# Cross-attention block of a perceiver kernel: the mask is prepared by ScalarE instead of VectorE and GpSimd, its first chunk laid by VectorE instead of a transfer, the context loaded in two halves

## The chip, the cores and the metric

The kernel runs on one core of a Trainium2 chip. The metric is the device time of one execution in microseconds; lower is better. The core has TensorE (PE in the rows, with its weight loads as PEld), VectorE (DVE), ScalarE (ACT), GpSimd (POOL) and SyncE (SP), which here only issues transfers.

## The reference, cut to what matters

For a batch of 32, `x` is 64 x 256 per entry and the context is 1601 x 256 per entry, float32. The model is a layer norm, masked cross-attention of `x` on the context with 16 heads of 16 columns, a residual; then causal self-attention with a gate; then a layer with 8 experts. The change touches the cross-attention alone:

```python
qp = (q @ Wq.T + bq).reshape(b, t_q, h, d // h).transpose(0, 2, 1, 3)
kp = (k @ Wk.T + bk).reshape(b, t_kv, h, d // h).transpose(0, 2, 1, 3)
vp = (v @ Wv.T + bv).reshape(b, t_kv, h, d // h).transpose(0, 2, 1, 3)
scores = jnp.einsum('bhqd,bhkd->bhqk', qp, kp) / jnp.sqrt(jnp.float32(d))
mask = (attention_mask == 1)[:, None, :, :]
scores = jnp.where(mask, -jnp.inf, scores)
attn = jax.nn.softmax(scores, axis=-1)
out = jnp.einsum('bhqk,bhkd->bhqd', attn, vp)
```

The mask is int32, 64 x 1601 per batch entry, with values 0 and 1; a position with 1 is excluded.

## The kernel before

**Blocks and periods.** The cross-attention is a software pipeline over the 32 batch entries, called blocks. In the period of block b each engine works on three blocks: scores, exponentials and values of block b; key and value projections and the maxima of block b+1; and the loading and splitting of the context and the mask of block b+2. Two periods form the body of a hardware loop (periods 2 to 29); the rest stands unrolled around it.

**Orders.** The order of work in a period is written by hand in five lists, one for each engine, and every engine works strictly in the order of its list. A letter is a kind of unit and the number says which one. On TensorE, S is half a tile of transposed scores (8 products; 13 tiles of up to 128 context rows make 26 units), K one of 8 key projections, M one of 16 products from which the maxima are taken, V one of 7 value projections (V6 has half the work), W the values of one tile (W11 and W12 also sum the weights, and W12 adds the sums that GpSimd made), T the turning of the maxima into a row, O the turning of the previous block's output. On ScalarE, E is the exponential of one S, KH and VH keep the results of K and V, CH makes the float16 high part of one of the four context chunks. On GpSimd, A1 to A10 add up the exponentials of tiles 0 to 10, CL makes the low part of a context chunk, QB spreads the queries, MQ makes the last chunk of the mask. On VectorE, X is the maximum of one M, KL the low part of K, SH gathers the maxima, SPR writes the row of shifts that every S of the block reads, MP makes the first three mask chunks, MA1 to MA3 copy mask chunk 1 to 3 into the stacked keys for all 16 heads, N normalizes the previous block and R adds the residual. On SyncE, CX loads the context and the mask, QR and QS bring the queries, MD0 lays mask chunk 0 by a transfer, ST0 and ST1 stack the two halves of the keys (17 transfers each).

**The places the change touches.** `mbias` holds the mask as bfloat16, minus 2^120 at a masked position and zero elsewhere, in two buffers. It is made by `prepare_mask` on VectorE (L517, columns 0 to 1151) and by `mask_tail` on GpSimd (L387, the last 449 columns). It is read twice: by every X (L496) and, as raw 16-bit numbers, by `lay_mask`, which copies 64 partitions of it into the stacked keys `kst`. Chunks 1 to 3 are copied by VectorE (L523) and chunk 0 by a transfer (L343).

The first S of a block waits for SPR (`qaug_ready`), for chunk 0 of the mask (`laid[0]`) and for the first half of the stacked keys. The first key projection K0 waits for all four CL of its block, and so for GpSimd's CL3 in the period before. `BANK` gives each unit its PSUM bank, and a unit waits until the unit that used the bank before has been read. M3 uses the banks of K3 and K4, so it waits for KL4, which waits for KH4; KH4 may overwrite the keys only when ST1 of the block before has landed.

## Time and profile before

| | |
|---|---|
| time, median of 3 runs | 2209.67 us (2206.32 to 2211.14) |
| time of the profiled execution | 2218.2 us |
| its span | 2216.4 us |
| start of the first and the last product of the values (L749), by the trace | 116.5 and 1563.3 us |
| busy in the steady stretch from 200 to 1400 us: PE, DVE, ACT, POOL | 1026.3, 867.9, 713.5, 959.1 us of 1200 |
| mean granted TensorE clock in that stretch | 0.93 |

The busy share of TensorE says little by itself, since its products overlap in the pipeline. The useful views here are the list of waits, which says what ended the idle time of an engine, and the timeline of each engine around the point where one period ends and the next begins. A releaser "issue" means that the engine waited for nothing that the profile shows.

### The profile page before, as it was taken

The page shows a single profiled execution, that of the slowest core. Times are in us where ns is not written, and L with a number is a line of the kernel's source. Part 1 is how long each engine was busy: PE and PEld are TensorE (multiplying, and loading weights), DVE is VectorE, ACT ScalarE, POOL GpSimd, SP SyncE. Part 2 cuts the span into 40 slices and gives each one's busy share as a digit, 9 for nine tenths or more (in the row PEclk, how much of TensorE's full clock was granted, in tenths as well). Part 3 has the DMA queues.
Part 4 walks back from the last instruction along what each step waited for, and adds up shares of the span by engine and source line. Part 5 has one row for each costly group of instructions (what it writes and reads, how often), then busy time and mean ns, then how long its engine had stood idle before and what let it go on. Part 6 is the DMA issues. An engine that isn't in the chain of part 4 may idle for free. (4 is left out here: it accounts for less than half of the span.)

```text
span 2216.4 us, 63044 instructions
## 1 busy us (share of the span) xinstructions
PE 1827.9 (82%) x24267; PEld 1300.9 (59%) x24267; DVE 1476.4 (67%) x3029; ACT 1124.7 (51%) x1815; POOL 1446.3 (65%) x714
## 2 busy tenths in 40 slices
PE   2687888888888888888888888888768787599996
PEld 1365656655666566655666555666435555388885
DVE  3676768766777776776777777778567776544442
ACT  2365655665666565555656566655354442133332
POOL 3387778877888787878778788886345541144442
PEclk9999999999999998989999999999885655699998
DMA  3567766677666776667766677664353333377774
GB/s 108 126 129 144 134 124 121 124 146 130 124 120 127 143 137 116 124 121 148 132 120 123 119 144 137 122 122 83 113 181 132 110 101 121 124 231 221 231 220 134
DMA packets 198496, 302.86 MB, mean 137 GB/s; under 512 B 60020, under 2 KB 166324, under 8 KB 197955
## 3 DMA queue, kind: packets, MB, share of 16 engines
q1 hardware_dynamic: 189412, 286.90, 58.7%
q0 software_dynamic: 8832, 12.06, 2.8%
q8 instruction: 223, 3.65, 0.8%
q14 instruction: 29, 0.24, 0.0%
HBM read 163.02 MB, written 31.98 MB: 88 GB/s over the span
## 5 line engine op out<-in xcount | busy, mean ns | idle before, releaser
L399 POOL TENSOR_TENSOR p_sum<-p_sum,pT 128x1024 f32<-128x1024 f32 x288 | 678.4, 2355 | 207.9 <-ACT pT L616 195.5
L616 ACT ACTIVATE pT<-scored,lift 128x512 f32<-128x512 f32 (+1 forms) x832 | 546.9, 684 | 206.3 <-PE scored L726 187.7
L496 DVE CUSTOM_DVE_ANT_0 junk<-key_ring,mbias 128x898 bf16<-128x898 f32 (+1 forms) x512 | 508.7, 1021 | 197.7 <-issue 197.3
L726 PE MATMUL scored<-qst,kst 128*128 128x64 f16 x6656 | 333.0, 199 | 105.0 <-issue 97.1
L726 PEld LDWEIGHTS scored<-qst,kst 128*128 128x128 f16 x6656 | 283.8, 103 | 206.1 <-issue 165.4
L373 POOL TENSOR_TENSOR cp<-cx,cp 128x768 f16<-128x768 f32 (+1 forms) x128 | 318.0, 2492 | 60.4 <-ACT cp L574 60.4
L692 PE MATMUL key_ring<-wvp,cp 128*128 128x256 f16 (+1 forms) x2496 | 317.3, 277 | 1.4 <-DVE kl L469 0.6
L603 ACT ACTIVATE kh<-key_ring,bks 128x384 f16<-128x384 f32 (+1 forms) x256 | 152.4, 595 | 252.6 <-PE key_ring L681 181.7
L692 PEld LDWEIGHTS key_ring<-wvp,cp 128*128 128x128 f16 (+1 forms) x2496 | 232.5, 100 | 59.2 <-issue 20.4
L749 PE MATMUL o_acc<-pT,v 128*32 128x128 f32 x6656 | 261.4, 288 | 2.1 <-DVE x_all L485 0.9
L469 DVE SCALAR_TENSOR_TENSOR kl<-key_ring,bks,kh 128x384 f16<-128x384 f32 (+1 forms) x256 | 162.4, 635 | 132.8 <-ACT kh L603 128.1
L523 DVE COPY kst<-mbias 64x6144 f16<-64x6144 f16 (+1 forms) x96 | 219.5, 2287 | 3.0
L681 PE MATMUL key_ring<-cp,wkr 128*128 128x384 f16 (+1 forms) x768 | 185.7, 382 | 31.8 <-issue 31.4
L749 PEld LDWEIGHTS o_acc<-pT,v 128*32 128x32 f32 x6656 | 174.3, 114 | 56.5 <-issue 31.6
L624 ACT ACTIVATE v<-key_ring 128x512 f32<-128x512 f32 (+1 forms) x224 | 125.7, 561 | 154.1 <-PE key_ring L692 154.1
L681 PE MATMUL key_ring<-cp,wkp 128*128 128x384 f16 x768 | 161.4, 350 | 36.0 <-POOL cp L373 33.9
L1558 POOL DMA_INDIRECT acc_d<-ys,to_row x46 | 74.8, 1625 | 158.8 <-DVE ys L1672 151.8
L1753 PE MATMUL score<-xp,w1p 128*128 128x256 f16 x1518 | 175.9, 275 | 2.3 <-DVE xp L1650 1.6
L984 POOL TENSOR_TENSOR w_parts<-w_whole,w_parts 128x1408 f16<-128x1408 f32 x24 | 70.8, 2957 | 140.9 <-ACT w_whole L1254 140.9
L1753 PEld LDWEIGHTS score<-xp,w1p 128*128 128x128 f16 x1518 | 147.6, 99 | 25.2 <-issue 7.5
L707 PE MATMUL key_ring<-kh,qh 32*128 32x384 f16 x512 | 119.3, 347 | 43.6 <-DVE kl L469 33.8
L681 PEld LDWEIGHTS key_ring<-cp,wkr 128*128 128x128 f16 x768 | 72.1, 106 | 92.0 <-issue 53.3
(224 smaller groups left out, 2438.6 us busy)
## 6 DMA issues: line engine op xcount, KB each, us to landing
cx<-in_ctxT SPq DMA_DIRECT2D x32, 1601.0 KB, 14.3
w1p<-wsp SPq DMA_DIRECT2D x23, 1408.0 KB, 8.5
msk<-in_mask SPq DMA_DIRECT2D x64, 400.2 KB, 14.0
kst<-mbias SPq DMA_DIRECT2D x32, 768.0 KB, 14.5
wsp<-w_parts SPq DMA_DIRECT2D x24, 704.0 KB, 3.7
w2p<-wsp SPq DMA_DIRECT2D x23, 640.0 KB
kst<-kh SPq DMA_DIRECT2D x256, 52.1 KB, 2.3
kst<-kl SPq DMA_DIRECT2D x256, 52.1 KB, 2.3
```

Source lines behind the costliest of these rows:

```text
L373: pool.tensor_tensor(cp[:, j, 1, :, chunk(n)], cx[:, :, chunk(n)], cp[:, j, 0, :, chunk(n)], ALU.subtract).then_inc(cl_ready, 1)
L399: pool.tensor_tensor(p_sum[:], p_sum[:], pT[:, u], ALU.add).then_inc(added, 1)
L469: dve.scalar_tensor_tensor(kl[:, t, chunk(c)], ring[:, BANK["K", k], 0:KWIDTH[c]], bks[:, c % 2, t:t + 1], kh[:, t, chunk(c)], ALU.add, AL ...
L496: dve.tensor_tensor_reduce(junk[:, n % 2, :, 0:MPAIR[half]], ring[:, at:at + 2, 0:MPAIR[half]], mbias[:, j, MS[2 * half]:MS[2 * half] + 2 ...
L523: dve.tensor_copy(kst[MASK_AT:P, :, chunk(c)], mbias[MASK_AT:P, j, MS[c]:MS[c] + KWIDTH[c]].bitcast(F16).unsqueeze(1).to_broadcast([S, H, ...
L603: act.activation(kh[:, t, chunk(c)], ring[:, BANK["K", k], 0:KWIDTH[c]], ACT.Identity, bias=bks[:, c % 2, t:t + 1]).then_inc(kh_kept, 1)
L616: act.activation(pT[0:n, u, HALF * half:HALF * half + HALF], scored[0:n, half, :], ACT.Exp, bias=lift[0:n, 0:1], scale=SSCALE).then_inc(ex ...
L681: mm = pe.matmul(ring[:, BANK["K", k], 0:KWIDTH[c]], (wkp, wkr)[c % 2][:, z, cc, P * t:P * t + P], cp[:, j, y, cc, chunk(c)], start=(cc == ...
L692: mm = pe.matmul(ring[0:n, BANK["V", u], D * half:D * half + D], cp[:, j, z, cc, P * kt:P * kt + n], wvp[:, y, cc, :], start=(cc == 0 and ...
L726: mm = pe.matmul(scored[0:n, half, S * (h % PAIRS):S * (h % PAIRS) + S], kst[:, place, rows], qst[:, j, h, :], start=True, stop=True, skip ...
L749: mm = pe.matmul(o_acc[STRIP * g:STRIP * g + STRIP, P * t:P * t + P], v[0:n, j, kt, STRIP * p:STRIP * p + STRIP], pT[0:n, u, P * p:P * p + ...
L1753: mm = pe.matmul(score[:, 2 * (g % 2) + bank, at], w1p[:, i % 2, c, z, P * block:P * block + P], xp[:, i % 2, y, c, :], start=(c == 0 and ...
```

## The change

The mask is kept with the other sign: plus 2^96 at a masked position, subtracted in X, with the sign of the constant in `delta` turned as well. ScalarE makes it in a unit MB: one instruction Abs(mask - 1) over all 1601 columns in place, then, after that has completed, two instructions Relu(2^96 - 2^96 * that) into `mbias`. MP on VectorE and MQ on GpSimd are gone. Chunk 0 is laid by VectorE as MA0, between SH and SPR, instead of by SyncE's MD0. CX becomes CX0 and CX1, one for each half of the columns, with a semaphore each; CX0 waits only for CL0 and CL1 of the previous use. The mask is loaded by a unit MK of its own after QS. The lists of all engines are rearranged, and some banks are dealt out anew.

```diff
-MASKED = float(2.0 ** 120)
+MASKED = float(2.0 ** 96)
...
-PE_ORDER = steps("S0 K0 S1 K1 O S2 S3 K2 S4 M0 W0 S5 K3 S6 M1 S7 K4 W1 S8 M2 S9 K5 M3 S10 S11 W2 M4 M5 S12 S13 K6 S14 W3 W4 M6 M7 K7 S15  "
-                 "S16 M8 M9 W5 W6 V0 S17 S18 M10 M11 V1 S19 W7 S20 M12 M13 W8 W9 S21 V2 S22 M14 M15 W10 S23 V3 S24 V4 S25 T V5 W11 W12  "
+PE_ORDER = steps("S0 S1 K0 K1 S2 S3 K2 M0 S4 O S5 K3 S6 K4 M1 S7 S8 W0 W1 M2 K5 S9 M3 S10 W2 W3 S11 M4 M5 S12 K6 S13 W4 M6 M7 S14 S15 K7  "
+                 "S16 W5 M8 M9 S17 S18 V0 W6 W7 M10 M11 S19 V1 S20 S21 M12 M13 W8 W9 S22 V2 S23 V3 M14 M15 S24 S25 W10 W11 V4 V5 T W12  "
                  "V6")
-ACT_ORDER = steps("E0 KH0 E1 KH1 E2 E3 E4 E5 KH2 E6 E7 KH3 KH4 E8 E9 KH5 E10 E11 E12 E13 KH6 E14 KH7 CH0 E15 E16 VH0 E17 E18 E19 VH1 E20  "
-                  "CH1 E21 VH2 E22 E23 CH2 VH3 E24 E25 VH4 VH5 CH3 VH6")
-POOL_ORDER = steps("QB A1 A2 A3 A4 A5 A6 A7 A8 CL0 A9 CL1 A10 CL2 CL3 MQ")
-DVE_ORDER = steps("N MA3 R KL0 X0 KL1 X1 KL2 KL3 KL4 X2 X3 KL5 X4 X5 KL6 X6 X7 KL7 X8 X9 X10 X11 X12 X13 MP X14 X15 SH MA2 SPR MA1")
-SP_ORDER = steps("CX QR QS MD0 ST0 ST1")
+ACT_ORDER = steps("E0 E1 KH0 KH1 E2 E3 KH2 E4 E5 E6 KH3 KH4 E7 E8 CH0 KH5 E9 E10 E11 E12 KH6 E13 E14 E15 KH7 E16 E17 E18 VH0 E19 E20 E21  "
+                  "CH1 VH1 E22 VH2 E23 CH2 E24 VH3 E25 CH3 VH4 MB VH5 VH6")
+POOL_ORDER = steps("QB A1 A2 A3 A4 A5 CL0 A6 A7 A8 A9 CL1 A10 CL2 CL3")
+DVE_ORDER = steps("MA3 N KL0 KL1 R X0 KL2 X1 KL3 KL4 X2 X3 KL5 X4 X5 KL6 X6 X7 KL7 X8 X9 X10 X11 X12 X13 MA2 X14 X15 SH MA0 MA1 SPR")
+SP_ORDER = steps("CX0 CX1 QS MK QR ST0 ST1")
...
-        ("T", 0): 2, ("V", 0): 4, ("V", 1): 4, ("V", 2): 4, ("V", 3): 4, ("V", 4): 0, ("V", 5): 4, ("V", 6): 1}
+        ("T", 0): 0, ("V", 0): 4, ("V", 1): 4, ("V", 2): 3, ("V", 3): 4, ("V", 4): 0, ("V", 5): 3, ("V", 6): 2}
...
-                    def load(b):
-
-                        after(sp, cl_ready, KC * b)
-                        sp.dma_start(cx[:], a["ctxT"][bass.ds(b, 1)].rearrange("o (c p) k -> p (o c) k", p=P)).then_inc(ctx_in, 16)
-                        after(sp, mask_ready, b)
-                        after(sp, tail_ready, b)
+                    def load(b, part):
+
+                        after(sp, cl_ready, KC * b + (2 * part + 2 - KC))
+                        sp.dma_start(cx[:, :, HALVES[part]],
+                                     a["ctxT"][bass.ds(b, 1), :, HALVES[part]].rearrange("o (c p) k -> p (o c) k", p=P)).then_inc(ctx_in[part], 16)
+
+                    def load_mask(b):
+
+                        after(sp, mask_ready, 2 * b)
                         for half in range(2):
                             sp.dma_start(msk[64 * half:64 * half + 64, :], a["mask"][bass.ds(b, 1)].rearrange("o q k -> (o q) k")).then_inc(mask_in, 16)
...
-                    def lay_mask(b, j, c):
-
-                        after(sp, st_done, HT * b + (2 * GT * (c + 1) - HT))
-                        if not has_later(b - 1):
-                            sp.wait_ge(mask_ready, b + 1)
-                        sp.dma_start(kst[MASK_AT:P, :, chunk(c)],
-                                     mbias[MASK_AT:P, j, MS[c]:MS[c] + KWIDTH[c]].bitcast(F16).unsqueeze(1).to_broadcast([S, H, KWIDTH[c]])).then_inc(laid[c], 16)
...
-                    def mask_tail(b, j):
-
-                        pool.wait_ge(mask_in, 32 * b + 32)
-                        after(pool, laid[KC - 1], b - 1)
-                        pool.tensor_tensor(hold_p[:], lift[0:1], lift[0:1], ALU.add)
-                        pool.tensor_scalar(mbias[:, j, MS[3]:NM], msk[:, KS[3]:NK], 1, -MASKED, ALU.is_equal, ALU.mult).then_inc(tail_ready, 1)
...
-                        if n % PAIRS == 0:
-                            dve.wait_ge((mask_ready, tail_ready)[n // PAIRS], b + 1)
+                        if n == 0:
+                            dve.wait_ge(mask_ready, 2 * b + 2)
...
-                                                 1.0, -3e38, ALU.add, ALU.max, mx[:, p, half:half + 1]).then_inc(m_read, 1)
+                                                 1.0, -3e38, ALU.subtract, ALU.max, mx[:, p, half:half + 1]).then_inc(m_read, 1)
...
-                    def prepare_mask(b, i, j):
-
-                        dve.wait_ge(mask_in, 32 * b + 32)
-                        after(dve, m_read, MUNITS * (b - 1))
-                        after(dve, laid[0], 16 * (b - 1))
-                        dve.tensor_scalar(mbias[:, j, 0:MS[2] + KWIDTH[2]], msk[:, 0:KS[3]], 1, -MASKED, ALU.is_equal, ALU.mult).then_inc(mask_ready, 1)
-
                     def lay_mask(b, j, c):
 
-                        dve.wait_ge(*((mask_ready, b + 1) if c < KC - 1 else (tail_ready, b + 1)))
+                        dve.wait_ge(mask_ready, 2 * b + 2)
...
+                        if n % 2 == 0:
+                            act.wait_ge(ctx_in[n // 2], b * 16 + 16)
                         if n == 0:
-                            act.wait_ge(ctx_in, b * 16 + 16)
                             after(act, v_done, VU * (b - 1))
...
+                    def prepare_mask(b, j):
+
+                        act.wait_ge(mask_in, 32 * b + 32)
+                        act.activation(msk[:].bitcast(F32), msk[:], ACT.Abs, bias=less_one[:, 0:1]).then_inc(mask_apart, 1)
+                        after(act, m_read, MUNITS * (b - 1))
+                        after(act, laid[KC - 1], b - 1)
+                        act.wait_ge(mask_apart, b + 1)
+                        for to, cols in ((0, slice(0, KS[3])), (MS[3], slice(KS[3], NK))):
+                            act.activation(mbias[:, j, to:to + cols.stop - cols.start], msk[:, cols].bitcast(F32), ACT.Relu, bias=masked[:, 0:1],
+                                           scale=-MASKED).then_inc(mask_ready, 1)
...
-                            pe.wait_ge(laid[c], b + 1 if c > 0 else b * 16 + 16)
+                            pe.wait_ge(laid[c], b + 1)
...
-    delta[-S:] = MASK_Q * np.eye(S)[:, None, None, :]
+    delta[-S:] = -MASK_Q * np.eye(S)[:, None, None, :]
```

## Rows read from the trace of the kernel before

**Rows 1.** The waits, whole span: us in total, times, longest us.
```profile
PE key_ring L681 <- POOL cp L373: 33.9, 18, 2.3
...
PE key_ring L707 <- DVE kl L469: 33.8, 14, 6.0
...
PE key_ring L681 <- issue: 31.4, 13, 3.4
```
**Rows 2.** PE's timeline from T to K0; start, duration, what, idle before.
```profile
982.79 0.61 PE L769 MATMUL key_ring<-minus,m 128*1 128x128 bf16 x8
983.33 1.48 PE L692 MATMUL key_ring<-wvp,cp 128*128 128x256 f16 x12
984.74 0.64 PE L749 MATMUL o_acc<-pT,v 128*32 128x128 f32 x16
...
985.64 0.62 PE L749 MATMUL o_acc<-pT,v 65*32 65x128 f32 x16
...
987.05 0.84 PE L692 MATMUL key_ring<-wvp,cp 128*65 128x256 f16 x6
987.73 0.40 PE L726 MATMUL scored<-qst,kst 128*128 128x64 f16 x8
990.40 1.69 PE L681 MATMUL key_ring<-cp,wkp 128*128 128x384 f16 x6 [2.27 <-POOL cp L373]
```
**Rows 3.** PE's timeline: inside K7, at S20, V6, first S after the loop's branch.
```profile
1011.39 0.91 PE L681 MATMUL key_ring<-cp,wkr 128*128 128x449 f16 x2 [2.46 <-issue]
...
1020.02 0.41 PE L726 MATMUL scored<-qst,kst 128*128 128x64 f16 x8 [0.40 <-ACT pT L616]
...
1032.18 0.84 PE L692 MATMUL key_ring<-wvp,cp 128*65 128x256 f16 x6
1035.43 0.60 PE L726 MATMUL scored<-qst,kst 128*128 128x64 f16 x8 [2.41 <-issue]
```
**Rows 4.** GpSimd's timeline: A10, CL2 with CL3, MQ; a CL0.
```profile
981.50 2.35 POOL L399 TENSOR_TENSOR p_sum<-p_sum,pT 128x1024 f32<-128x1024 f32 x1
983.80 6.54 POOL L373 TENSOR_TENSOR cp<-cx,cp 128x768 f16<-128x768 f32 x2
...
990.46 2.87 POOL L387 TENSOR_SCALAR mbias<-msk 128x449 bf16<-128x449 int32 x1
...
1020.30 1.67 POOL L373 TENSOR_TENSOR cp<-cx,cp 128x768 f16<-128x768 f32 x1
```
**Rows 5.** VectorE's timeline: SH, MA2, SPR, MA1.
```profile
982.11 0.17 DVE L504 TENSOR_REDUCE m<-mx 128x8 bf16<-128x16 f32 x1
982.31 3.15 DVE L523 COPY kst<-mbias 64x6144 f16<-64x6144 f16 x1
985.50 1.21 DVE L509 TENSOR_SCALAR qst<-key_ring 1x1024 f16<-1x1024 f32 x1
986.74 1.86 DVE L523 COPY kst<-mbias 64x6144 f16<-64x6144 f16 x1
```
**Rows 6.** ScalarE's groups by form: busy us, mean ns, idle before.
```profile
L574 ACT ACTIVATE cp<-cx 128x768 f16<-128x768 f32 x96 | 80.2, 837 | 2.8 <-DMA cx<-in_ctxT 2.8
...
L574 ACT ACTIVATE cp<-cx 128x898 f16<-128x898 f32 x32 | 30.3, 946 | 0.0
```
**Rows 7.** VectorE's groups by form: X of the second half, MP.
```profile
L496 DVE CUSTOM_DVE_ANT_0 junk<-key_ring,mbias 128x898 bf16<-128x898 f32 x256 | 269.7, 1087 | 95.4 <-issue 95.2
...
L517 DVE TENSOR_SCALAR mbias<-msk 128x1152 bf16<-128x1152 int32 x32 | 67.1, 2096 | 0.0
```
**Rows 8.** Line 1301, the self-attention's exponential: ns min/median/max.
```profile
L1301 ACT ACT_TABLE_LOAD  x7: 1283/1283/1283, 1652.0 to 1803.0; - x7
```
**Rows 9.** SyncE's timeline: the context's load.
```profile
994.97 0.40 SPq L302 DMA_DIRECT2D cx<-in_ctxT  x1
```
**Rows 10.** The page's transfers: KB each, us from issue to landing.
```profile
cx<-in_ctxT SPq DMA_DIRECT2D x32, 1601.0 KB, 14.3
...
kst<-mbias SPq DMA_DIRECT2D x32, 768.0 KB, 14.5
```

More of the change, by code:

```diff
@@ L217, in program @@
             lift = sb1("lift", [P, 1])
-            hold_p = sb1("hold_p", [1, 1])
+            less_one = sb1("less_one", [P, 1])
+            masked = sb1("masked", [P, 1])
             hold_v = sb1("hold_v", [P, 2])
@@ L227, in program @@
             xw = pT[:, 0:2].rearrange("p s (c k) -> p s c k", c=DC)
-            ctx_in, ch_ready, cl_ready = sem("ctx_in"), sem("context_high_ready"), sem("context_low_ready")
+            ctx_in = [sem(f"ctx_in{j}") for j in range(2)]
+            ch_ready, cl_ready = sem("context_high_ready"), sem("context_low_ready")
             wp_high, wp_ready = sem("weights_high_parts"), sem("weight_parts_ready")
-            mask_in, mask_ready, tail_ready = sem("mask_in"), sem("mask_ready"), sem("mask_tail_ready")
+            mask_in, mask_apart, mask_ready = sem("mask_in"), sem("mask_less_one"), sem("mask_ready")
             laid = [sem(f"mask_laid{c}") for c in range(KC)]
             q_done, qh_kept, q_kept = sem("q_done"), sem("qh_kept"), sem("q_kept")
-            init_done, N_INIT = sem("init_done"), 6
+            init_done, N_INIT = sem("init_done"), 8
             k_done, kh_kept, k_kept = sem("k_done"), sem("kh_kept"), sem("k_kept")
@@ L348, in period @@
                             if kind == "CX" and has_later(b):
-                                load(b + 2)
+                                load(b + 2, n)
+                            elif kind == "MK" and has_later(b):
+                                load_mask(b + 2)
                             elif kind == "QS" and do_b:
@@ L355, in period @@
                                 stack_keys(b + 1, n)
-                            elif kind == "MD" and do_b:
-                                lay_mask(b + 1, 1 - j, n)
                     sp.wait_ge(init_done, N_INIT)
-                    load(0)
+                    for part in range(2):
+                        load(0, part)
+                    load_mask(0)
                     sp.wait_ge(q_kept, DC * NCH)
@@ L406, in period @@
                                 low_context(b + 2, j, n)
-                            elif kind == "MQ" and has_later(b):
-                                mask_tail(b + 2, j)
                             elif kind == "QB" and has_later(b):
@@ L420, in _ @@
                     pool.wait_ge(q_kept, DC * NCH)
-                    mask_tail(0, 0)
                     prepare_queries(0, 0, 0)
@@ L426, in _ @@
                 def _(dve):
-                    dve.memset(mbias[:, :, MS[2] + KWIDTH[2]:MS[3]], -MASKED).then_inc(init_done, 1)
+                    dve.memset(mbias[:, :, MS[2] + KWIDTH[2]:MS[3]], MASKED).then_inc(init_done, 1)
                     dve.memset(hold_v[:], 0.0).then_inc(init_done, 1)
@@ L433, in _ @@
                     dve.memset(lift[:], LIFT).then_inc(init_done, 1)
+                    dve.memset(less_one[:], -1.0).then_inc(init_done, 1)
+                    dve.memset(masked[:], MASKED).then_inc(init_done, 1)
                     dve.wait_ge(x_in, 16)
@@ L544, in period @@
                                 lay_mask(nb, nj, n)
-                            elif kind == "MP" and has_later(b):
-                                prepare_mask(b + 2, i + 1, j)
                     dve.wait_ge(q_kept, DC * NCH)
-                    prepare_mask(0, 0, 0)
                     periods(dve, period)
@@ L636, in period @@
                                 high_context(b + 2, j, n)
+                            elif kind == "MB" and has_later(b):
+                                prepare_mask(b + 2, j)
+                    act.wait_ge(init_done, N_INIT)
+                    prepare_mask(0, 0)
                     periods(act, period)
```

## The prediction

> **What bounds the kernel now.** The list of waits comes first. TensorE is busy 1026 of the 1200 us of the steady stretch, so what matters is what ends its idle time. Three entries there concern this change [rows 1]: K0 waits for GpSimd's last low part, 33.9 us in 18 times; M3 waits for VectorE's KL, 33.8 us in 14 times; and there are waits that nothing in the profile explains. The timelines of two neighbouring boundaries between periods show where they stand. Going from an even block to an odd one, S0 follows V6 at once, then K0 stands still for 2.27 us until CL3 ends [rows 2, 4]. Going from an odd block to an even one, at the loop's branch, S0 itself starts 2.41 us late for no reason shown, and K0 does not wait afterwards [rows 3]. A third kind is a gap in the middle of one unit, 2.46 us within K7 [rows 3], where no semaphore is waited for: I read it, and the one at the branch, as instructions that are not there yet. The change does not shorten the program, so I leave them as they are.
>
> So in this stretch TensorE's own order sets the pace, and the tail of GpSimd's list sets it at every second boundary. GpSimd does A10, CL2 and CL3 back to back from 981.50 to 990.34 us [rows 4], and K0 starts at 990.40.
>
> **Part 1, what is removed.** MQ costs GpSimd 2.87 us [rows 4], but it stands behind CL3, and GpSimd then waits for exponentials anyway; worth 0. MP costs VectorE 2.10 us on average [rows 7], between X13 and X14; its place is taken by MA2, worth about 0. The transfer MD0 moves 768 KB and lands after 14.5 us [rows 10]; nobody waits for it, since its block starts a whole period later. Less traffic may shorten the waits for the stacked keys (part 4).
>
> **Part 2, GpSimd's tail.** One of the low parts moves out of it: a CL0 of 1.67 us [rows 4] now comes after A5. Also, S21 now stands next to S20, ahead of M12, M13, W8 and W9. From S20 to the end of V6 there were 13.0 us [rows 3], and by the count of products the new S21 ends some 12 us before S0's place at 987.73 [rows 2], at 975.7. An exponential and CH1 of 0.84 us [rows 6] end near 977.3. Then come CL1 1.67, A10 2.35, CL2 1.67 and CL3 near 1.9 (the last from 1.67 by its columns): 984.9 with nothing in between. K0 now stands behind S1, so it is due at 988.1. The margin is 3.2 us where 2.27 us were missing.
>
> What eats this margin is VectorE's copies. The row shows it: MA2 is asked for at 982.31, while A10 runs to 983.85, and takes 3.15 us; MA1, of the same shape, takes 1.86 us [rows 5]. MA2 ends 1.61 us after A10. CL2 and CL3 together take 6.54 us where a CL alone takes 1.67 [rows 4]. So each copy that meets GpSimd stops it for about 1.6 us, or is stopped by it. Three copies (MA2, MA0, MA1) would bring CL3 to 989.7, so between 0 and 1.6 us of K0's wait may stay. Since S0 is late in the same case (part 3), I take all 33.9 us as gone.
>
> The Trainium skill (SBUF — State Buffer, Who interferes with whom) says that a VectorE copy in a two-port mode and a GpSimd instruction take one shared pair of ports as an exclusive lock for the whole instruction, in order of issue. The trace agrees with it in MA2's 3.15 us. It speaks against a fourth copy at this place.
>
> **Part 3, VectorE before SPR.** Before, SH at 982.11 was followed by MA2 and SPR, and SPR ended at 986.71, about 1.0 us ahead of S0 [rows 2, 5]. Now MA0 and MA1 both stand between SH and SPR. M15 comes earlier in TensorE's new order: behind it are two S and W10 (1.1 us, an estimate from W11 without its sums), W11 0.90, V4 and V5 2.82, T 0.54, W12 1.41 and V6 0.68 [rows 2], 7.45 us in all. It ends at 980.3, X14 and X15 of 1.05 us each (269.7 over 256) [rows 7] end near 982.3 and SH near 982.5. T ends at 985.6, so the copies are what SPR waits for. With nothing in the way: 982.5 + 2 x 1.86 + 1.21 = 987.4 [rows 5], just in time for S0 at 987.73. If one copy waits out one CL of 1.67 us, SPR ends at 989.1 and S0 starts 1.3 us late. If both do, it is 990.7 and 3.0 us late. CL2 and CL3 run just there, and I take one, 1.3 us. At the branch, S0 is late by 2.41 us anyway [rows 3], which hides 1.3 us. There are 16 boundaries without a branch: +20.8 us, bounds 0 and 48.
>
> **Part 4, the waits in front of M3.** M3 waits for KL4, and KH4 for the landing of ST1. S25, which lets ST1 start, now has W10 and V4 behind it too, so it comes some 1.9 us earlier against S0 [rows 2], K4 is earlier in the list, and the traffic is lighter. That would remove the 33.8 us [rows 1]. But where M3 does not wait, gaps of the third kind turn up nearby, so I take a third, -11.3 us, bounds 0 and -33.8.
>
> **Part 5, ScalarE.** The trace has no Abs and no Relu. The nearest rows are the copies of 768 and 898 columns, 0.837 and 0.946 us [rows 6], 0.84 ns a column. That gives 1.54 us for 1601 columns, 1.16 for 1152 and 0.57 for 449, in sum 3.3 us. They stand between VH4 and VH5. Behind them wait VH5, VH6 and E0. V4 ends 4.0 us before S0's place (V5, T, W12 and V6 follow [rows 2]), VH4 0.6 us later (from the same 0.84 ns a column), MB 3.3 us after that, VH5 another 0.6 us: 0.5 us behind S0's place. K0, which needs V5's bank, is due 0.7 us behind S0. So the cover is thin: 0.2 us if S0 is on time, 1.5 us with S0 1.3 us late as in part 3. I take 0. If ScalarE were late by more, K0 would wait for the rest. A change of function tables would cost 1.28 us each [rows 8], up to 2.6 us in a period: above the cover by 1.1 us at 16 boundaries, 18 us. No such load stands between Copy, Identity and Exp in the cross-attention, so 18 us is only the bound.
>
> The Trainium skill (ScalarE: Activation LUTs, Table sets: the hidden batching unit) says that relu and abs are in every set. By it, the price is 0; no trace so far shows it for these two.
>
> **Part 6, the context in halves.** CX was issued at 994.97, 4.6 us after CL3 had ended at 990.34 [rows 4, 9], because SyncE had first to issue ST1. So the earlier release of a half buys nothing. What it does buy is that CH0 needs only half of the transfer. CH0 moves from after KH7 to after E8, some 13 us behind S0; the load is issued about 5.5 us behind S0 and half of 14.3 us [rows 10] makes 12.7. That just fits: 0, bound +1 us in each of 30 periods. The extra issue of 0.40 us [rows 9] is hidden.
>
> **Part 7, the start.** ScalarE makes the first mask with nothing to hide it, 3.3 us, and MA0 of 1.86 us [rows 5] stands before the first SPR; about one K covers 1.1 us of it: +4.0 us.
>
> **The sum.** -33.9 + 20.8 - 11.3 + 4.0 = -20.4 us. Against the profiled execution's own 2218.2 us that is 2197.8. The median of the runs is 8.5 us lower, 2209.7, so the forecast there is 2189.3, and I write 2189, 0.9% faster.
>
> **Rivals.** *VectorE's chain becomes the bound (slower).* At each boundary both copies lose to CL2 and CL3. S0 is 3.0 us late without the branch and 0.6 us later than now with it: 16 x 3.0 + 15 x 0.6 = 57; minus 33.9 and nothing for M3, plus 4: +27, 2237. It decides from the point where SPR ends 2.3 us behind V6. For it: the copies stand in exactly the stretch where GpSimd has no pause [rows 4]. Against it: GpSimd's tail is shorter, so A10 and CL2 may be over before MA0. Half-way, with S0 2.15 us late without the branch and 0.3 us with it, it is 34.4 + 4.5 - 33.9 + 4.0 = +9.0, 2219. The rule of the shared ports that the Trainium skill gives (SBUF — State Buffer, Who interferes with whom) is this rival's mechanism.
>
> *All of it comes free.* Copies find GpSimd idle, M3's wait goes whole: -33.9 - 33.8 + 4 = -64, and 2146; with half of part 3's price, 2156. For it: 3.2 us of margin. Against: three copies in a row.
>
> *Nothing moves.* What K0 and M3 stop waiting for turns up as gaps of the third kind, whose places depend on the order: -20 + 20 = 0, 2210. For it: they are the largest entry in TensorE's idle time, and 31.4 us of them stand in K units alone [rows 1].
>
> **Chances.** Forecast 0.44 (its own range 2172 to 2204), all free 0.18, VectorE the bound 0.23, nothing moves 0.15. The range leaves out the ends of the second and third: 2156 to 2222. A measurement of this kernel can tell about 0.2% from no change. Faster: 0.44 + 0.18 and a little of the last, 0.63; within: 0.14; slower: 0.23.
>
> **What the profile would show.** Part 2 is right if K0's wait for GpSimd is gone from the waits. Part 3 is right if S0 behind V6 waits about 1.3 us for VectorE at every second boundary. Part 4: M3's wait for KL is near 22 us. Part 5: ScalarE's new instructions take 3.3 us, with no table load between them. Part 6: CH0 has no wait for the context. The prediction is wrong if S0 waits 3 us, if K0 waits for VH5, or if the unexplained gaps change by more than 20 us.

## The result, and the profile after

The changed kernel takes 2142.93 us in the median of 4 runs (2126.50 to 2155.97), the kernel before 2210.4 us in 4: a ratio of 0.967 over their fast runs, 95% interval 0.958 to 0.977, so 3.3% faster (the medians themselves stand at 0.969). Forecast were 2189 us and a range from 2156 to 2222. The sign was right and the size was not: more than three times the gain came, and the median lies outside the range. The profiled execution took 2138.41 us, its span is 2136.6 us, 79.8 us shorter than that of before.

The page's head after the change:

```profile
span 2136.6 us, 63160 instructions
...
PE 1792.0 (84%) x24267; PEld 1280.2 (60%) x24267; DVE 1543.1 (72%) x3031; ACT 1225.2 (57%) x1911; POOL 1420.9 (67%) x650
```

The list of waits after it, in the columns of [rows 1]:

```profile
PE scored L723 <- DVE qst L500: 83.0, 28, 3.8
...
PE scored L723 <- issue: 47.7, 26, 3.7
...
ACT cp L556 <- DMA cx<-in_ctxT: 17.8, 18, 2.0
...
ACT kh L585 <- DMA kst<-kst: 12.2, 10, 2.1
...
PE key_ring L678 <- issue: 7.0, 9, 1.4
PE key_ring L678 <- POOL cp L372: 6.1, 2, 3.2
```

K0's wait for GpSimd fell from 33.9 to 6.1 us, and M3's wait for KL, 33.8 us before, is not in the list any more. In their place stands one new wait, which is now TensorE's largest: S0 for SPR (L500), 83.0 us. And the gaps without a shown reason, which the forecast held fixed, fell most: 97.1 us in S units and the 31.4 us in K units of [rows 1] made 128.5, and now there are 47.7 + 7.0 = 54.7.

Two kinds have to be kept apart in this sum. The stops of S0 behind the loop's branch were 33.1 us in 13 times; now 8.5 us in 3 times are left under this name, since S0 waits for SPR at the same place. At all other places there were 95.4 us, and there are 46.2: they fell by 49 us.

What these gaps are can be read from the trace. The page's third part has a queue of the kind "instruction":

```profile
q8 instruction: 223, 3.65, 0.7%
```

The trace has the time of each of its packets, 16,384 bytes apiece, 5.8 in a period, so one in 7 to 8 us. In the cross-attention TensorE has 47 stops of over 0.3 us without a reason before, those of S0 left out, and 33 after. Every one of them ends 1.2 to 1.9 us after the end of such a packet, and every stop at the branch 1.9 to 2.2 us after one. In all 18 traces of this document it is 493 stops, 1.2 to 2.4 us after a packet, and 150 stops of S0, 1.8 to 2.7 us after one. So TensorE waits there for its next instructions.

The busy time of TensorE is 1792.0 us for the same 24267 products, where it was 1827.9 (the page of before). The steady stretch from 200 to 1400 us shows where part of this comes from, first before, then after (us, then busy time and instructions of PE, PEld, DVE, ACT, POOL, the granted clock, the transfers' share, GB/s):

```profile
200.00:1400.00 1200.00, 1026.27 (x15734) 722.20 (x15733) 867.85 (x1713) 713.54 (x1167) 959.12 (x440) 0.93 0.70 129
```

```profile
200.00:1400.00 1200.00, 1058.80 (x16774) 748.73 (x16773) 980.85 (x1827) 844.37 (x1325) 1008.17 (x415) 0.95 0.61 120
```

By busy time over products, one takes 1026.27/15734 = 65.2 ns before and 1058.80/16774 = 63.1 ns after, at a mean granted clock of 0.93 and 0.95 of 2.4 GHz. The timeline of TensorE at one boundary without a branch shows where the clock is lost:

```profile
846.40 0.84 PE L689 MATMUL key_ring<-wvp,cp 128*65 128x256 f16 x6
850.46 1.03 PE L723 MATMUL scored<-qst,kst 128*128 128x64 f16 x16 [3.21 <-DVE qst L500]
851.30 2.11 PE L678 MATMUL key_ring<-cp,wkp 128*128 128x384 f16 x6
...
858.11 1.14 PE L678 MATMUL key_ring<-cp,wkr 128*128 128x384 f16 x6
```

K0, two S units behind the 3.21 us of idle, takes 2.11 us, and six products of the same shape take 1.14 us further on. The granted clock was 0.50 from 851.3 to 853.5 us and 1.00 from 858.1 to 859.3 us. So such a gap costs its length and again 1 us or more in the products behind it. Not every one does: at 980.96 us, behind 2.76 us of idle, the clock stayed at 1.00 and K0 took 1.14 us. From the first block's S0 to the last one's, TensorE worked 177 us at the half clock before and 125 us after. Half of the difference, 26 us, is the clock's part of the 36 us of busy time, by estimate; the rest stays open.

The same boundary on VectorE, then on GpSimd:

```profile
842.44 0.17 DVE L495 TENSOR_REDUCE m<-mx 128x8 bf16<-128x16 f32 x1
842.64 6.34 DVE L507 COPY kst<-mbias 64x6144 f16<-64x6144 f16 x2
849.01 1.21 DVE L500 TENSOR_SCALAR qst<-key_ring 1x1024 f16<-1x1024 f32 x1
```

```profile
838.49 3.89 POOL L391 TENSOR_TENSOR p_sum<-p_sum,pT 128x1024 f32<-128x1024 f32 x1
842.33 5.03 POOL L372 TENSOR_TENSOR cp<-cx,cp 128x768 f16<-128x768 f32 x2
```

SH is over at 842.61, as near to S0's place (847.24, the end of V6) as the forecast had it: 4.6 us ahead against 5.2. But MA0 and MA1 together take 6.34 us, where a free one takes 1.86 [rows 5]. CL2 starts 0.3 us before MA0 and takes its usual 1.66 us. Then MA0, CL3 and MA1 take turns, and each waits out the one in front: they are recorded with 2.96, 3.43 and 3.46 us. SPR ends at 850.22, 3.0 us behind V6. A10, in front, took 3.89 us instead of 2.35, since MA2 had gone ahead of it.

The exclusive lock on the shared pair of ports, of which the Trainium skill speaks (SBUF — State Buffer, Who interferes with whom), fits all of these durations.

The mask on ScalarE, its timeline from VH4's end to E0, and its groups by form:

```profile
843.86 1.62 ACT L590 ACTIVATE msk<-msk,less_one 128x1601 f32<-128x1601 int32 x1
845.51 1.82 ACT L595 ACTIVATE mbias<-msk,masked 128x1152 bf16<-128x1152 f32 x2
847.23 0.84 ACT L617 ACTIVATE v<-key_ring 128x512 f32<-128x512 f32 x2
851.25 1.27 ACT L609 ACTIVATE pT<-scored,lift 128x512 f32<-128x512 f32 x2 [3.19 <-PE scored L723]
```

```profile
L590 ACT ACTIVATE msk<-msk,less_one 128x1601 f32<-128x1601 int32 x32 | 51.9, 1622 | 0.0
L595 ACT ACTIVATE mbias<-msk,masked 128x1152 bf16<-128x1152 f32 x32 | 40.2, 1256 | 1.2
L595 ACT ACTIVATE mbias<-msk,masked 128x449 bf16<-128x449 f32 x32 | 20.9, 654 | 0.0
```

It takes 1.62 + 1.26 + 0.65 = 3.5 us by the means, 3.3 were forecast, and it is over before S0 can start. There is no table load in the cross-attention: the trace has one at 1 us and the next at 1556 us.

### The profile page after: what moved, and what is told of

Read it like the earlier page. It is cut to its first block and busy times, and to the rows that moved or that the text cites. A ratio compares the mean times of both kernels' runs of the same rounds, so it can differ in the third digit from the quotient of the medians.

```text
span 2136.6 us, 63160 instructions
## 1 busy us (share of the span) xinstructions
PE 1792.0 (84%) x24267; PEld 1280.2 (60%) x24267; DVE 1543.1 (72%) x3031; ACT 1225.2 (57%) x1911; POOL 1420.9 (67%) x650
## 5 line engine op out<-in xcount | busy, mean ns | idle before, releaser
L391 POOL TENSOR_TENSOR p_sum<-p_sum,pT 128x1024 f32<-128x1024 f32 x288 | 702.0, 2438 | 61.1 <-ACT pT L609 44.8
L723 PE MATMUL scored<-qst,kst 128*128 128x64 f16 x6656 | 318.4, 198 | 141.0 <-DVE qst L500 83.0
L723 PEld LDWEIGHTS scored<-qst,kst 128*128 128x128 f16 x6656 | 266.8, 102 | 242.9 <-issue 185.9
L507 DVE COPY kst<-mbias 64x6144 f16<-64x6144 f16 (+1 forms) x128 | 347.3, 2733 | 3.0
L689 PE MATMUL key_ring<-wvp,cp 128*128 128x256 f16 (+1 forms) x2496 | 305.0, 273 | 4.8 <-DVE mx L487 3.8
L746 PE MATMUL o_acc<-pT,v 128*32 128x128 f32 x6656 | 240.1, 278 | 2.1 <-issue 1.1
L746 PEld LDWEIGHTS o_acc<-pT,v 128*32 128x32 f32 x6656 | 169.9, 110 | 24.4 <-issue 8.7
L388 POOL TENSOR_TENSOR p_sum<-pT 128x1024 f32<-128x1024 f32 x32 | 75.4, 2355 | 164.1 <-ACT pT L609 164.1
L678 PE MATMUL key_ring<-cp,wkp 128*128 128x384 f16 x768 | 171.8, 367 | 8.1 <-POOL cp L372 6.1
L981 POOL TENSOR_TENSOR w_parts<-w_whole,w_parts 128x1408 f16<-128x1408 f32 x24 | 69.8, 2917 | 140.6 <-ACT w_whole L1251 140.6
```

The costliest lines, as they stand in the source:

```text
L391: pool.tensor_tensor(p_sum[:], p_sum[:], pT[:, u], ALU.add).then_inc(added, 1)
L507: dve.tensor_copy(kst[MASK_AT:P, :, chunk(c)], mbias[MASK_AT:P, j, MS[c]:MS[c] + KWIDTH[c]].bitcast(F16).unsqueeze(1).to_broadcast([S, H, ...
L678: mm = pe.matmul(ring[:, BANK["K", k], 0:KWIDTH[c]], (wkp, wkr)[c % 2][:, z, cc, P * t:P * t + P], cp[:, j, y, cc, chunk(c)], start=(cc == ...
L689: mm = pe.matmul(ring[0:n, BANK["V", u], D * half:D * half + D], cp[:, j, z, cc, P * kt:P * kt + n], wvp[:, y, cc, :], start=(cc == 0 and ...
L723: mm = pe.matmul(scored[0:n, half, S * (h % PAIRS):S * (h % PAIRS) + S], kst[:, place, rows], qst[:, j, h, :], start=True, stop=True, skip ...
L746: mm = pe.matmul(o_acc[STRIP * g:STRIP * g + STRIP, P * t:P * t + P], v[0:n, j, kt, STRIP * p:STRIP * p + STRIP], pT[0:n, u, P * p:P * p + ...
```

## The experiments

Ratios are to the kernel before, run on the same chip. "Gaps without a reason" are TensorE's idle times with the releaser "issue". The medians of the kernel before were 2210.6 to 2215.4 us in these series; where two kernels ran on different chips, their ratios are the better comparison.

**spr_early**

```diff
-... X14 X15 SH MA0 MA1 SPR
+... X14 X15 SH MA0 SPR MA1
```

> The changed kernel with VectorE's MA1 moved behind SPR (order SH MA0 SPR MA1). After the change S0 waits for SPR 83.0 us in 28 waits, about 3.2 us at nearly every boundary, behind two copies that took 6.34 us together where one alone takes 1.86. Theory A (those copies are what S0 waits for, and TensorE has no other bound close behind): SPR comes about 3.2 us earlier, the wait falls below 15 us, the kernel gains 50 to 75 us against the changed one, near 2080 us. Theory B (the wait only covers something else that is due at the same time: VH5 behind the mask on ScalarE, CL3 on GpSimd, the stop at the loop's branch of 2.4 us): the wait moves to K0 or to S0 without a reason shown, and the gain is under 25 us, 2120 us or more.

Measured 2126.78 us, ratio 0.965 (0.959 to 0.971). S0's wait for SPR is gone (1.1 us are left), but this stands in the waits instead:

```profile
PE scored L723 <- issue: 81.5, 40, 3.1
...
PE key_ring L678 <- POOL cp L372: 37.5, 14, 5.0
```

K0 waits for GpSimd again, more than before the change, and the stops at the branch, which the wait for SPR had covered, show again: 33.0 us in 13 times. The other gaps without a reason grow from 46 to 60 us. Theory B holds: the wait had covered things that are due almost at the same time. The intervals of the two ratios overlap, so no gain is shown.

**chunk0_by_transfer**: the changed kernel, chunk 0 laid by SyncE as before.

```diff
-SP_ORDER = steps("CX0 CX1 QS MK QR ST0 ST1")
+SP_ORDER = steps("CX0 CX1 QS MK QR MD0 ST0 ST1")
-... SH MA0 MA1 SPR
+... SH MA1 SPR
```

> The changed kernel with mask chunk 0 laid by SyncE's transfer of 768 KB as before, and no MA0 on VectorE; everything else as after the change. Theory A (what the change gained in gaps without a reason came from the lighter traffic): the gaps inside S15, S9 and K7 and the wait of M3 come back, 40 to 60 us; SPR comes 3 us earlier, which gives 50 to 75 back; about even, 2115 to 2150 us. Theory B (the gaps went with the new order of units, the traffic has no part in it): only the gain of SPR stays, 2070 to 2095 us.

Measured 2146.09 us, ratio 0.972 (0.968 to 0.977). It is even with the changed kernel, as theory A had it. S0's wait for SPR is gone; K0 waits 28.5 us for GpSimd, and ScalarE waits for the stacked keys, 62.7 us where it was 12.2:

```profile
ACT kh L595 <- DMA kst<-kst: 62.7, 27, 7.8
```

The nearest kernel is spr_early, which also has one copy between SH and SPR and ran on the same chip: 2126.78 us, 29.5 us of this wait, and 17.2 us of S units waiting for ScalarE, where here there are 42.3. So the transfer costs some 19 us in this list, though the two intervals overlap a little, and it costs them behind the stacked keys: M3's wait does not come back, and the gaps without a reason away from the branch are 66 us against 60.

**mask_by_two**: the changed kernel, mask by VectorE and GpSimd.

```diff
-... X12 X13 MA2 X14      (VectorE)     ... CL2 CL3       (GpSimd)   ... VH4 MB VH5   (ScalarE)
+... X12 X13 MP MA2 X14   (VectorE)     ... CL2 CL3 MQ    (GpSimd)   ... VH4 VH5      (ScalarE)
```

> The changed kernel with the mask made by VectorE (1152 columns, behind X13) and GpSimd (449 columns, behind CL3) again instead of by ScalarE. Theory A (moving the mask mattered little, since ScalarE's 3.3 us and GpSimd's 2.9 us both lay beside other work): VectorE's chain to SPR grows by 2.1 us in front of X14, of which a part shows as a longer wait of S0, 5 to 65 us slower than the changed kernel, 2150 to 2205 us. Theory B (ScalarE's mask stands in the way of VH5 and E0, hidden behind S0's wait): ScalarE's time is given back and the kernel is within 10 us of the changed one, 2133 to 2153 us.

Measured 2176.96 us, ratio 0.984 (0.978 to 0.990). That is theory A: 34 us slower than the changed kernel's 2142.93, 40 us slower than its 2137.42 on this chip. V4 needs the bank of M14, and X14 now stands behind MP and MA2:

```profile
PE scored L731 <- DVE qst L513: 76.1, 24, 3.8
PE key_ring L697 <- DVE mx L500: 57.3, 27, 2.4
```

(The two rows are of the steady stretch.) In the changed list the mask's 2.1 us on VectorE have no cover, and ScalarE's 3.5 us were over before anything needed them. What MQ alone costs was not separated.

**after_traffic**

```diff
+sp.dma_start(spare_d[:], qh_all[MASK_AT:P, 0, 0:KWIDTH[0]].unsqueeze(1).to_broadcast([S, H, KWIDTH[0]])).then_inc(spare_in, 16)
```

> The changed kernel with a transfer of 768 KB in each period that nobody waits for, in the place of the removed one, from the queries to a spare place in memory in the same pieces of 768 bytes. Theory A (traffic delays TensorE's instructions and the stacked keys): the gaps without a reason grow from 50 us in the steady stretch towards the 96 us of before, and the time with its clock by 40 to 70 us, 2180 to 2215 us. Theory B (traffic has no part): within 10 us of the changed kernel, 2133 to 2153 us.

Measured 2141.37 us, ratio 0.970 (0.964 to 0.975); gaps without a reason 46.6 + 10.2 = 56.8 us. In the changed kernel 768 KB more per period at this place cost nothing: theory B. It is a milder load than MD0, though. It is issued 13.1 us behind S0 and lands after 9.4 us, while MD0 in chunk0_by_transfer is issued at 14.5 us and takes 13.8 us, and ScalarE waits only 15.0 us for the stacked keys here.

**orders_only**: the kernel before with the new lists and banks alone (MP in front of MA2, MQ behind CL3, MD0 and one CX as before, no MB, no MA0).

> The kernel before with the lists of TensorE, ScalarE, VectorE and GpSimd and the banks of the changed one, and nothing else of the change: the mask by VectorE (in front of MA2) and GpSimd (behind CL3), chunk 0 by the transfer, the context in one piece. Theory A (the order of the units is what took away M3's wait and the gaps without a reason): most of the gain is there, minus what VectorE's mask costs in front of X14 (34 us, as mask_by_two against the changed kernel), 2150 to 2185 us. Theory B (the order matters little and needs the lighter engines and queues): 2190 us or more.

Measured 2283.78 us, ratio 1.029 (1.025 to 1.033). It is slower than the kernel before. The number lies in theory B's range, which was open above, but neither theory expected a loss. The largest reason is in ScalarE's waits, where before there were 2.8 us for the context, and in what follows on TensorE:

```profile
ACT cp L574 <- DMA cx<-in_ctxT: 209.2, 31, 9.6
...
PE scored L726 <- ACT pT L616: 200.2, 53, 8.3
```

CH0 stands after E8 in the new list, and there the whole context has not landed. E9 and S11 stand behind it; 163 of the 200 us are in front of S11.

**one_load**: the changed kernel, CH0 waits for both halves.

```diff
-if n % 2 == 0:
-    act.wait_ge(ctx_in[n // 2], b * 16 + 16)
 if n == 0:
+    for part in range(2):
+        act.wait_ge(ctx_in[part], b * 16 + 16)
```

> The changed kernel with the context still loaded in two transfers, but CH0 waits for both of them, as it had to with one. Theory A (the load in halves is what lets CH0 stand after E8, and orders_only was slow for the lack of it: there ScalarE stood 165 us for the context): ScalarE waits for the context in front of nearly every E9, S11 stands still behind it, 100 to 160 us slower than the changed kernel, 2240 to 2300 us. Theory B (orders_only was slow for its mask in front of X14 and the transfer of chunk 0): ScalarE waits little, within 20 us of the changed kernel.

Measured 2224.77 us, ratio 1.006 (1.003 to 1.010), beside 2137.42 us and 0.968 (0.963 to 0.972) of the changed kernel on the same chip (after_again): 87 us, in kind theory A, a little less than its range. Of the 3.3% nothing is left. TensorE stands still in front of S11 instead, 106 us, and with that the gaps without a reason nearly vanish, 6.3 + 3.1 us.

```profile
ACT cp L556 <- DMA cx<-in_ctxT: 141.1, 31, 7.8
```

**before_light**

```diff
-sp.dma_start(cx[:], a["ctxT"][bass.ds(b, 1)]...
+n = NK if isinstance(b, int) and b == 0 else 48
+sp.dma_start(cx[:, :, 0:n], a["ctxT"][bass.ds(b, 1), :, 0:n]...
```

> The kernel before, but after the first block each load of the context brings 48 of the 1601 columns (about 50 KB instead of 1.6 MB), so later blocks compute with the first one's context elsewhere; the time of all engines' work is unchanged. Theory A (the gaps inside S9, K7, S15 and S20, which the profile gives no reason for, come because TensorE's next instructions arrive behind the bulk transfers, and M3's wait because the stacked keys do): of 97.1 and 31.4 us without a reason some 35 us stay, those at the loop's branch; M3's 33.8 us fall below 10; 60 to 120 us faster with the clock, 2090 to 2150 us. Theory B (these gaps belong to the program's length and order and not to traffic): the gaps stay within 20 us and the time within 25 us of before.

All loads behind the first bring 3% of the context, and the later blocks compute with the first one's elsewhere.

Measured 2083.15 us, ratio 0.939 (0.934 to 0.944): 132 us faster, past the range of theory A. The gaps in K units are not in the list any more. In S units this is left, 34.2 of the 55.7 us at the branch, and M3's wait is 7.3 us:

```profile
PE scored L727 <- issue: 55.7, 31, 2.9
PE key_ring L682 <- POOL cp L374: 41.9, 18, 3.1
```

**after_light**: the same in the changed kernel, 48 columns of each half.

> The changed kernel with each load of a context half cut to 48 columns after the first block (the results of later blocks are made from the first one's context elsewhere). Theory A: the gaps without a reason behind S15, K5 and S11 (50 us in 28 periods) go, the wait of S0 for SPR stays; 30 to 60 us faster than the changed kernel, 2080 to 2115 us. Theory B: gaps stay; within 15 us of the changed kernel.

Measured 2082.85 us, ratio 0.941 (0.938 to 0.945), 60 us faster than the changed kernel.

```profile
PE scored L724 <- DVE qst L501: 105.1, 31, 3.6
...
PE scored L724 <- issue: 2.4, 6, 0.7
```

The two light kernels take the same time within 0.3 us. Without the bulk of the context's transfers the change is worth nothing: what it takes from K0 and the branch it gives back at S0. Its 3.3% show only where the work lies beside those transfers.

The instruction packets say how. The one that is due at S15 in even blocks, the first to begin later than 13 us behind that block's S0, begins 20.8 us behind it in the kernel before and 14.8 us in before_light (medians of 14 blocks). In the changed kernel it is 17.4 us and in after_light 15.2 us. In the kernel before, the context's load lands at 21.3 us; in the changed one, its second half lands at 17.7 us.

**before_small_md0**

```diff
-sp.dma_start(kst[MASK_AT:P, :, chunk(c)], mbias[...].bitcast(F16).unsqueeze(1).to_broadcast([S, H, KWIDTH[c]]))
+sp.dma_start(kst[MASK_AT:P, 0:1, chunk(c)], mbias[...].bitcast(F16).unsqueeze(1))
```

> The kernel before with its transfer of mask chunk 0 cut to one head of 16, 48 KB instead of 768 KB (the other heads of chunk 0 keep zeros, so masked positions there are not excluded). Theory A (that transfer prolongs the stretch in which TensorE's instructions come late, and the change gained by its removal): the gaps inside K7 (31.4 us in 28 periods), S15 and S20 (28 us) go, those inside S9 stay, 25 to 70 us faster than before. Theory B (it costs nothing, as the extra transfer in after_traffic did): within 10 us of before.

Measured 2185.03 us, ratio 0.989 (0.986 to 0.993), 26 us faster: at the lower edge of theory A in size. K7's gap did not go: in the steady stretch K units still have 29.5 us without a reason, where they had 30.4, while M3's wait fell from 23.6 to 9.4 us. So the step that the theory named was the wrong one, and the packet in front of S15 is hardly earlier, 20.4 us. The stacked keys profit: ScalarE's wait for them fell from 69.8 to 40.8 us. Only one head of 16 gets chunk 0 of the mask here, so masked positions there count in the others.

**before_mask_later** and **after_mask_first**: the place of the mask's load, in both kernels.

```diff
-SP_ORDER = steps("CX QR QS MD0 ST0 ST1")            # before; CX loads the mask too
+SP_ORDER = steps("CX QR QS MK MD0 ST0 ST1")
-SP_ORDER = steps("CX0 CX1 QS MK QR ST0 ST1")        # changed
+SP_ORDER = steps("CX0 CX1 MK QS QR ST0 ST1")
```

> The kernel before with the mask's load moved behind the queries (CX QR QS MK MD0). Theory A: the gaps inside S9 and K7, 67.6 us in 28 periods, fall by 20 us or more, 20 to 50 us faster than before. Theory B: within 8 us of before, 0.3% to either side.

> The changed kernel with the mask's load directly behind the context's two, ahead of the queries (CX0 CX1 MK QS QR). Theory A (2.4 MB issued at once hold back TensorE's instructions for longer than 1.6 MB and then 0.8 MB, and the change gained by putting the queries between them): the gaps inside K5 and S15 grow by 20 us or more in 28 periods, 20 to 40 us slower than 2140. Theory B (the place of the mask's load has no part): within 8 us.

In the kernel before, the later load gives 2190.57 us, ratio 0.988 (0.983 to 0.993), 22 us faster. The packet in front of S15 begins at 17.5 instead of 20.8 us. The gaps in K units fall from 31.4 to 8.0 us, and those at S15 from 16.9 to 0.4; part of it comes back at S20, 34.7 us where there were 10.1:

```profile
PE scored L732 <- issue: 96.2, 38, 3.3
...
PE key_ring L687 <- issue: 8.0, 5, 2.5
```

In the changed kernel the earlier load gives 2149.28 us, ratio 0.967 (0.962 to 0.973). The ratio is that of the changed kernel itself, so no loss is shown, though its profiled execution has 57.4 instead of 47.7 us in S units. The packet in front of S15 begins at 17.7 us, where it was 17.4.

**shifted_pages**

```diff
+if j == 0:
+    for _ in range(SPARE_WAITS):        # 60
+        pe.wait_ge(init_done, N_INIT)
```

> The changed kernel with 60 waits on TensorE at the start of every even block that are long satisfied; they do no work. Theory A (the gaps stand at fixed places of the instruction stream, some 240 instructions of product and weight load apart, and mean that the next stretch of instructions isn't there): the gaps that stood behind the fifth product of S15 and the third of K5 in even blocks, and the second of S15 in odd ones, move some 30 products forward, into S13 or W4 and into W0; their sum stays within 20 us. Theory B (they belong to what S15 and K5 wait for): they stay where they are.

Measured 2138.57 us, ratio 0.966 (0.960 to 0.972). The gaps moved. In even blocks of the changed kernel one stands inside S14/S15, with 13 of 16 products in front of it (first row, a short one; 11 of them make 20.8 us). Now none is left there, and one stands inside W4, 5 of 16 products in front (second row, of this kernel, of the same block):

```profile
999.65 0.25 PE L723 MATMUL scored<-qst,kst 128*128 128x64 f16 x3 [0.17 <-issue]
```

```profile
1000.38 0.63 PE L747 MATMUL o_acc<-pT,v 128*32 128x128 f32 x11 [1.19 <-issue]
```

By the new list that is 28 products earlier, and nothing that W4's sixth product could wait for is new. In odd blocks it is the same: from the third product of S15 to the third of W4. In the loop of both kernels, before and after, the places within one block lie 118 to 122 products apart, or twice that, and each product has a weight load. So the gaps belong to places in the instruction stream: theory A. With the packets and before_light it says what they are: TensorE has used up its instructions, and the next ones arrive late while bulk transfers are under way.

Theory A's second part did not come: away from the branch the gaps should have kept their sum within 20 us, and only 15 of 47 us are left. The 60 waits lengthen S0's stop in even blocks from 3 to over 6 us, about 45 us in sum, and the time is the same. Like one_load, this kernel has few gaps because TensorE stands still elsewhere in the period. A shorter list of gaps is therefore no gain by itself.

The rule that the Trainium skill gives fits this (Runtime: NRT & Kernel Launch, Instruction fetch mechanics): instructions are fetched in blocks of 256 by the engine's own transfers. The distance of some 120 products with their weight loads, and the waits between them, agrees. It calls the cost mostly hidden; here it was not, by the 95.4 and 46.2 us.

**spr_early_k_by_half**

```diff
-if k == 0:
-    pe.wait_ge(cl_ready, b * KC + KC)
+if k % (KPROJ // 2) == 0:
+    pe.wait_ge(cl_ready, b * KC + (KC if k else 2))
```

> spr_early, and K0 waits for the low parts of chunks 0 and 1 only, which are all that K0 to K3 read, and K4 for all four. In spr_early K0 waits 32.0 us for GpSimd's last CL, in 12 waits. Theory A (that wait is the bound that took S0's place): it goes, 2085 to 2105 us. Theory B (something else, VH5 behind the mask or VectorE's KL chain, is due at the same time): K0 or K3 waits for that instead, 2115 us or more.

Measured 2122.60 us, ratio 0.958 (0.954 to 0.962), the lowest ratio found. Its interval lies just below that of after_again (0.963 to 0.972), and overlaps that of the first series (0.958 to 0.977). K0's wait went; in the steady stretch O waits for N instead:

```profile
PE o_acc L759 <- DVE att L468: 32.7, 15, 3.0
```

**norm_first**: N ahead of MA3 again.

> spr_early_k_by_half with N ahead of MA3 on VectorE, as in the kernel before. There O waits 32.7 us for the normalization, which stands behind MA3's copy of 2 us. Theory A (that is now the bound in front of O): the wait goes, 20 to 35 us faster than 2122.6. Theory B (TensorE waits for its instructions right after instead, since the page behind K1 is due 8 us later whatever is in front): S9 or K5 take the gap, within 10 us.

Measured 2120.50 us, ratio 0.961 (0.957 to 0.965). O's wait is gone, K3 waits 27.3 us for KL0 instead (steady stretch), and the time is the same: neither theory's gap, but theory B's time.

**late_ma3**: MA3 behind X0.

> norm_first with MA3 behind X0 instead of behind N. In norm_first K3 waits 27.3 us for KL0, behind MA3's 2 us. Theory A (MA3 is what it waits for): that wait goes, 10 to 25 us faster, 2095 to 2110 us. Theory B (K3 is early and another wait follows, for its instructions or for the exponentials): 2113 us or more.

Measured 2133.79 us, ratio 0.963 (0.958 to 0.968), no gain. That is theory B. K3's wait fell to 3.2 us, and the M units behind X0 wait for VectorE:

```profile
PE key_ring L704 <- DVE mx L487: 51.2, 35, 3.2
```

**after_again** is the changed kernel in a second series.

> The changed kernel as it is, on the chip of the three others of this call, for comparison with them: 2130 to 2155 us, 0.96 to 0.975 of the kernel before.

It took 2137.42 us, ratio 0.968 (0.963 to 0.972).

## Why the prediction was right or wrong

The terms against the profiled executions (us):

| term | forecast | measured |
|---|---|---|
| K0 waits for GpSimd | -33.9 | 33.9 to 6.1: -27.8 |
| S0 waits for SPR | +20.8 | 83.0 |
| M3 waits for KL | -11.3 | -33.8 |
| gaps without a reason | 0 | 128.5 to 54.7: -73.8 |
| TensorE's busy time | 0 | 1827.9 to 1792.0: -35.9 |
| start of the first values | +4.0 | 116.5 to 124.5: +8.0 |
| sum | -20.4 | -80.3 (span: -79.8) |

That the measured column closes is no proof of causes: busy and idle time of TensorE make up the span whatever ended the waits. The rows of S0 and of the gaps also share the stops at the branch. Taken by place, S0 waited 35.6 us for all reasons before and 91.5 us after, +55.9, and the other gaps are -49.2.

**The step that failed** is the last sentence of the first part: that the third kind of gap belongs to the program's length and is to be left as it is. It stands in the sum as 0. I had read it rightly as instructions that are not there yet, and the packets and shifted_pages bear that out. But when they arrive depends on the transfers, which before_light shows, and whether TensorE is there first depends on the lists. The gaps' own -73.8 us hold 24.6 us at the branch, which now lie under S0's wait; so 49 us are real. With fewer idle times goes part of the 36 us of busy time, for which the sum had no term at all, though the profile of before showed the price: it lists K units of 1.69 and 2.10 us behind a gap and 1.14 us elsewhere.

**The right sign was luck.** The terms that the sum did have, measured, are -27.8 for K0, +55.9 for S0, -33.8 for M3 and +8.0 for the start: +2.3 us, no gain. All of the gain is in the two terms that were put at nothing. It is luck too that the rival "all of it comes free" had 2146 us: it needs copies that find GpSimd idle, and they did not.

**Part 1**, MD0 worth nothing: wrong in the kernel before, 26 us by before_small_md0, and likely in the changed one, some 19 us by chunk0_by_transfer against spr_early. MP for MA2 worth nothing: that exchange was not tested by itself; with MP in front of MA2 and MQ back, the new list loses 34 us.

**Part 2**, K0's wait: right in size, but not by the margin of 3.2 us. In spr_early, where S0 is not late, K0 waits 37.5 us for GpSimd, longer than the 33.9 us of before. The wait was covered by S0's, not removed. GpSimd's A10 and its CL wait for VectorE's copies as priced.

**Part 3**, SPR: its mechanism was right, its size mis-sized. I took one collision of two, 1.3 us, and both happen, 3.0 us. Without the branch S0 waits 41.2 us in 15 times, inside the bound of 48. With the branch it waits 50 us where it was 36, so the branch hides most of it but not all. In the list both stand under SPR: 83.0 us in 28 waits. The rival "VectorE's chain becomes the bound" had this wait nearly and was still wrong in its sum, for want of the two missing terms.

**Part 4**, M3: all of it went, not a third. It stays away in chunk0_by_transfer and in orders_only too, so the new lists removed it, not the missing transfer. ScalarE's wait for the stacked keys fell from 69.8 us (waits of before) to 12.2. Of this, chunk 0 is worth some 33 us (62.7 against 29.5 in spr_early). Another 17 us is the difference between spr_early and the changed kernel, where S0 starts later.

**Part 5**, ScalarE: right, 3.5 us for 3.3, hidden, no table load. The cover was thinner than written: K0 was put 0.7 us behind S0 here and 0.4 us in part 2, and with 0.4 the 0.2 us of cover are gone. S0's long wait made room.

**Part 6**, the halves: CH0 was to have no wait and waits 17.8 us in 18 times, inside the bound of 30; S units wait for ScalarE 10.0 us where they waited 4.5. But "worth 0" misses what the halves do. With CH0 waiting for both, the new lists cost 87 us (one_load). Whether halves would gain with the old lists was not run; here they are the condition under which the lists can be changed.

**The rivals' frame** was too narrow as well: "all of it comes free" was given the gaps' present size as a floor, and ended at 2146.

**What stays open.** Two parts of the change help the kernel before by 22 and 26 us (the mask's load behind the queries; chunk 0's transfer cut to a sixteenth). The first, undone in the changed kernel, costs nothing that its interval shows, and the packet in front of S15 hardly moves there, 17.7 us for 17.4, where it moved from 20.8 to 17.5 in the kernel before. Why the mask's load delays it in one kernel and not in the other is not shown. The second was undone only together with a copy less in front of SPR. Nor is it shown why a packet is late: the trace has its time, not when it was asked for. How much the order itself contributed was not separated either: with the context awaited in one piece it loses.

## What to carry to other kernels

A gap in the middle of a unit that waits for nothing is not a constant of the program. Compare its end with the packets of the instruction queue, if the trace has them. Try the kernel once with its bulk loads cut to a sliver: here that said at once that 130 of 2210 us hang on traffic. Price every gap with the slower products behind it. When several engines end a period together, ask for each removed wait which one it had covered; here S0, the branch, K0 and O took turns, and removing 83 us of waiting gave 16 us at most, which the intervals do not separate from nothing.

## What the runs showed of the hardware

TensorE stood still at fixed places of its instruction stream for 0.3 to 3.9 us, and each stop ended 1.2 to 2.4 us after a packet of the instruction queue. Cutting the context's transfers took the stops in S and K units from 95 us to 22 in the kernel before, those at the branch left out, and from 46 to 2 in the changed one. Behind the hardware loop's branch, TensorE stopped for about 2.5 us in 13 passes of the kernel before, and cutting the transfers did not change that (34.2 us). The VectorE copies and GpSimd instructions that met here did not share but took turns: two copies of 1.86 us each when free took 6.34 us between and behind two CL of 1.67 us. Abs, Relu, Copy, Exp and Identity alternated on ScalarE without a table load.
